# A language-model block on one core: FFN weights prepared in SBUF and turned by DMA in block 0, whose down products go by parts, with block 0's attention in slots of its own

## The reference

```python
h = rms_norm(rms_norm(emb_table[ids], norm_weight) @ proj_weight.T, None)
# attention, 16 heads of 32
z = layernorm(h)
q, k = feature_map(z @ Wq.T) * 32**-0.5, feature_map(z @ Wk.T)    # layernorm over 32, gamma, beta
v = z @ Wv.T
attn = where(causal, einsum(q, k) ** 2, 0)
h = h + (attn @ v / (attn.sum(-1) + eps)) @ Wo.T
# FFN, 2048 wide; fwht is the Walsh-Hadamard transform
x = fwht(layernorm(h) * SU_ug) / 64
x = silu(x @ W_gate.T * (Ws_gate * 64)) * (x @ W_up.T * (Ws_up * 64))
h = h + fwht(x * SU_dp) / 64 @ W_down.T * (Wscale_dp * 64)
```

## Time and profile before

| | |
|---|---|
| median of three executions | 1368.69 us |
| the profiled execution | 1369.22 us |
| its span, first to last instruction | 1367.4 us |
| mean granted TensorE clock | 0.970 |
| PE busy | 1258.8 us (92%) |
| DVE busy | 658.7 us (48%) |
| POOL busy | 565.2 us (41%) |
| ACT busy | 397.9 us (29%) |
| under 512 B, of 232708 DMA packets | 197893 |

### The profile page before, as it was taken

One profiled execution on the slowest core, in us unless ns is written; L12 is line 12 of the kernel. 1 busy time (PEld: TensorE's weight loads), 2 busy tenths in 40 slices (PEclk: granted clock), 3 DMA queues, 4 the chain that ended last, 5 costly groups with the idle time before them and its releaser, 6 DMA issues.

```text
span 1367.4 us, 18781 instructions
## 1 busy us (share of the span) xinstructions
PE 1258.8 (92%) x7257; PEld 620.6 (45%) x7257; DVE 658.7 (48%) x1154; ACT 397.9 (29%) x703; POOL 565.2 (41%) x483
## 2 busy tenths in 40 slices
PE   5565398999999999999999999999999999999999
PEld 3453054554444444444444444444444444444444
DVE  2654558782645363545455445534553644361110
ACT  5452354442133212330233113311331133211210
POOL 0443244342266424752375227632664266421210
PEclk9797699999999999999999999999999999999999
DMA  9912313311435234423444244333543445020000
GB/s 307 318 24 62 78 36 65 70 26 37 100 101 109 47 93 108 106 57 85 101 108 70 70 101 108 83 67 90 115 86 55 100 101 108 16 70 24 0 0 31
DMA packets 232708, 113.97 MB, mean 83 GB/s; under 512 B 197893, under 2 KB 215609, under 8 KB 232121
## 3 DMA queue, kind: packets, MB, share of 16 engines
q1 hardware_dynamic: 220160, 74.38, 25.7%
q0 software_dynamic: 11520, 37.76, 9.4%
q10 hardware_dynamic: 952, 0.75, 0.2%
HBM read 57.01 MB, written 9.70 MB: 49 GB/s over the span
## 4 chain that ended last, share of the span: by engine, by line
PE 77%; DVE 9%; DMA 4%; issue 4%; ACT 4%; POOL 1%; SPq 0%; DVEq 0%; POOLq 0%; ACTq 0%
PE bank L1178 23%; PE bank L1179 23%; PE bank L1180 23%; PE bank L1330 3%; DMA prod<-sg 2%; PE bank L1173 2%; DVE wd L568 1%; PE bank L1221 1%; DVE wd L567 1%; DVE wgu L553 1%; DVE prod L765 1%; PE bank L1171 1%; DMA hid<-in_L_tok_norm_weight 1%; PE bank L1339 1%; ACT wgu L951 1%
## 5 line engine op out<-in xcount | busy, mean ns | idle before, releaser
L1178 PE MATMUL bank<-xT,wgu 128*128 128x512 f16 x1024 | 389.8, 381 | 1.4 <-DVE xT L804 1.4
L1179 PE MATMUL bank<-xT,wgu 128*128 128x512 f16 x1024 | 389.8, 381 | 0.0
L1180 PE MATMUL bank<-xT,wgu 128*128 128x512 f16 x1024 | 389.8, 381 | 0.0
L470 POOL TENSOR_TENSOR hid<-a,hid 128x512 f16<-128x512 f32 x128 | 172.9, 1350 | 284.4 <-ACT hid L951 284.1
L839 DVE SCALAR_TENSOR_TENSOR a<-bank,kap,sg 128x512 f32<-128x512 f32 x128 | 96.1, 751 | 313.6 <-PE bank L1180 296.1
L1178 PE MATMUL bank<-wd,hid 128*128 128x512 f16 x512 | 194.1, 379 | 0.0
L1180 PE MATMUL bank<-wd,hid 128*128 128x512 f16 x512 | 194.0, 379 | 0.0
L1179 PE MATMUL bank<-wd,hid 128*128 128x512 f16 x512 | 194.0, 379 | 0.0
L951 ACT ACTIVATE hid<-a 128x512 f16<-128x512 f32 x128 | 80.9, 632 | 278.8 <-DVE a L839 278.8
L1180 PEld LDWEIGHTS bank<-xT,wgu 128*128 128x128 f16 x1024 | 100.5, 98 | 121.9 <-issue 2.0
L1178 PEld LDWEIGHTS bank<-xT,wgu 128*128 128x128 f16 x1024 | 100.8, 98 | 117.7 <-DVE xT L804 2.3
(11 more groups left out here) (192 smaller groups left out, 1371.1 us busy)
## 6 DMA issues: line engine op xcount, KB each, us to landing
out<-a SPq DMA_DIRECT2D x24, 256.0 KB, 2.2
wgu<-in_L_ffn_W_gate SPq DMA_DIRECT2D x16, 256.0 KB, 6.6
wgu<-in_L_ffn_W_up SPq DMA_DIRECT2D x16, 256.0 KB, 5.1
wd<-in_L_ffn_W_down SPq DMA_DIRECT2D x4, 1024.0 KB, 9.3
out<-h_row SPq DMA_DIRECT2D x8, 256.0 KB, 2.0
hid<-att_table,ids_p POOLq DMA_INDIRECT x84, 3.5
xT<-in_L_tok_proj_weight SPq DMA_DIRECT2D x1, 1024.0 KB, 7.3
p<-in_L_attn_Wq SPq DMA_DIRECT2D x1, 1024.0 KB, 11.9
```

Of the source, the lines that this page charges most:

```text
L470: nc.gpsimd.tensor_tensor(hid[:, 1, s, :], a32[:, :], hid[:, 0, s, :], ALU.subtract)\
L1178: mm(dst, w[0], v[0], start=first, stop=False)
L1179: mm(dst, w[0], v[1], start=False, stop=False)
L1180: return mm(dst, w[1], v[0], start=False, stop=final)
```

## The change

- **Loads.** One DMA per group of gate or up weights with 2 KB runs takes the place of four with 512 B runs. `norm_w` is asked for before the projection, and the down weights' first tile after all gate and up weights. The layout of `wgu` is new.
- **Start.** The squares and the sum for Wo and its turned units, and the values' product, move from before attention 0 into its slots. So do the first steps of `down_mix`, to behind its last slot. The first head's product waits for the first low table half alone (`att_low`), not for all four.
- **Attention 0** has SLOTS0 = 18 slots of its own. The four sums of heads are turned by eight PE transposes and one ACT copy (O_FLIP_AT0) and not by DMA. Behind slot 17, `tail` makes the Wo rows, the norms and the mixes of the four row tiles with nothing between them, and the rows too are turned on the PE (`x_flip`, `x_copied`).
- **Gate and up units.** 12 of 32 (TURNED) are still turned by PE, in slots 1 to 12 of attention 0, through three banks. The others are made in slots 0 to 9 of FFN 0, two per slot, with no PE work. ACT scales the f32 rows in place and copies the high half into one of three stage buffers (RING), POOL subtracts for the low half (`unit_low`), SP turns both halves by one DMA transpose straight into `wgu`. A unit waits until the DMA of three units before has landed. The PE waits for a slot's two units before it uses them.
- **Down units.** ACT makes the high half, DVE the low half, a DMA transpose on the same ring turns them, the PE makes the Hadamard product as two f16 matmuls (`down_hada`), and ACT and DVE split the result one slot later. They lie in slots 9 to 23.
- **Banks.** Gate has two banks in FFN 0 too, up has two up to slot 9 and one from slot 10 on.
- **FFN 0's down products** go part by part of the 2048 columns (outer) over the four row tiles (inner). The rows' last sums come in slots 29 to 31 and behind.
- **Attention 1** picks its heads by matmul as attention 0 does. Gathers begin with block 2.

```diff
-BEFORE = 16
-UNITS_IN_SLOT = (0, 0) + (1,) * BEFORE + (0,) * 14
-UNITS_BESIDE = 16
...
+RING = 3
+TURNED = 12
+UNIT_AT = tuple(range(1, 13))
...
+MIXED_BEFORE = 4
+MIX_BESIDE = (2, 3, 4, 5, 6, 7, 8, 8, 9, 10, 11, 12)
+SPLIT_BESIDE = (9, 10, 11, 13, 13, 13, 14, 14, 14, 15, 15, 15, 16, 16, 17, 18)
+HADA_BESIDE = (10, 11, 12, 14, 15, 16, 16, 17, 17, 18, 18, 19, 19, 20, 21, 22)
...
+HEADS_AT0 = (4, 8, 12, 16)
+O_AT0 = (5, 9, 13, 16)
+O_FLIP_AT0 = (6, 10, 14, 17)
+SLOTS0 = 18
...
+        def landed(x):
+
+            if x < TURNED:
+                return S["st_lo"], x + 1
+            return turning(x), 16 * ((x - TURNED) // RING + 1)
...
-                for i in range(4):
-                    rows_of_tile = w[512 * g + P * i:512 * g + P * i + P, :].rearrange("p (k d) -> p k d", k=DC)
-                    nc.sync.dma_start(raw[n][:, :, i, :], rows_of_tile).then_inc(S[f"gu_land{n}"], 16)
+                rows_of_tile = w[512 * g:512 * g + 512, :].rearrange("(i p) d -> p i d", p=P)
+                nc.sync.dma_start(raw[n], rows_of_tile).then_inc(S[f"gu_land{n}"], 16)
...
+            def unit_turn(x):
+                if x < UNITS:
+                    sp.wait_ge(S["st_low"], x - TURNED + 1)
+                else:
+                    sp.wait_ge(S["st_lo"], x - UNITS + TURNED + 1)
+                nc.sync.dma_start_transpose(unit_home(x), stage_of(x).rearrange("p l d -> p (l d)"))\
+                    .then_inc(turning(x), 16)
...
+            def unit_low(x):
+                pool.wait_ge(S["st_hi"], x + 1)
+                nc.gpsimd.tensor_tensor(stage_of(x)[:, 1, :], unit_raw(x), stage_of(x)[:, 0, :], ALU.subtract)\
+                    .then_inc(S["st_low"], 1)
...
                 feed(0, s)
+                for x in units_beside(s):
+                    unit_low(x)
                 product(1, s)
                 attend(1, s)
-                if s == NORM_BESIDE:
...
+            def unit_low(x):
+                dve.wait_ge(S["st_hi"], x + 1)
+                if x < TURNED:
+                    n, i = unit_place(x)
+                    nc.vector.tensor_tensor(wgu[:, n, i, 1, :, :].rearrange("p k f -> p (k f)"), TURN[x % 3][:, :],
+                                            wgu[:, n, i, 0, :, :].rearrange("p k f -> p (k f)"), ALU.subtract)\
+                        .then_inc(S["st_lo"], 1)
+                else:
+                    nc.vector.scalar_tensor_tensor(stage_of(x)[:, 1, :], unit_raw(x), unit_scale(x), stage_of(x)[:, 0, :],
+                                                   ALU.mult, ALU.subtract).then_inc(S["st_lo"], 1)
...
+            def tail():
+                for m in range(4):
+                    row_sum(0, m)
+                    if m:
+                        x_low(0, m - 1)
+                    if m > 1:
+                        xT_low(0, m - 2)
+                    row_norm(0, m)
+                    if m == 0:
+                        pair_norm(2)
+                        half_terms(0)
+                    if m == 1:
+                        pair_scale(2)
+                        bound_low(0)
+                    if m == 2:
+                        half_scale(0)
+                    if m == 3:
+                        pair_norm(3)
+                xT_low(0, 2)
+                x_low(0, 3)
+                down_mix(MIXED_BEFORE - 1)
+                xT_low(0, 3)
+                pair_scale(3)
...
+            for s in range(SLOTS0):
+                product(0, s)
+                if s < 2:
+                    att_low(2 + s)
+                if s == 2:
+                    val_low()
+                for x in units_before(s - 1):
+                    unit_low(x)
+                if s - 1 in WO_UNIT_AT:
+                    wo_low(WO_UNIT_AT.index(s - 1))
+                for x in units_before(s + 1):
+                    unit_diagonal(x)
+                attend_first(s)
+                if s == 5:
+                    pair_norm(1)
+                if s == 7:
+                    pair_scale(1)
+                if s == 8:
+                    wo_terms()
+                if s == 9:
+                    wo_total()
+                if s == 11:
+                    wo_fit()
+            for k in range(MIXED_BEFORE - 1):
                 down_mix(k)
...
+            def unit_high(x):
+                if x < TURNED:
+                    n, i = unit_place(x)
+                    act.wait_ge(S["turned"], x + 1)
+                    copy(wgu[:, n, i, 0, :, :].rearrange("p k f -> p (k f)"), TURN[x % 3][:, :]).then_inc(S["st_hi"], 1)
+                    return
+                if x >= TURNED + RING:
+                    act.wait_ge(*landed(x - RING))
+                else:
+                    act.wait_ge(S["wo_ready"], 1)
+                if x < UNITS:
+                    act.wait_ge(S["gu_scaled"], x // 8 + 1)
+                    copy(unit_raw(x), unit_raw(x), scale=unit_scale(x)).then_inc(S["st_scaled"], 1)
+                    act.wait_ge(S["st_scaled"], x - TURNED + 1)
+                    copy(stage_of(x)[:, 0, :], unit_raw(x)).then_inc(S["st_hi"], 1)
+                else:
+                    act.wait_ge(S["d_mix"], 4 * min(x - UNITS, 3) + 4)
+                    act.wait_ge(S["bound_done"], 1)
+                    copy(stage_of(x)[:, 0, :], unit_raw(x), scale=unit_scale(x)).then_inc(S["st_hi"], 1)
...
-                for v in down_evicts(2 * s):
+                feed(0, s, GATE[s % 2])
+                for x in units_beside(s):
+                    unit_high(x)
+                for v in down_hadas(s - 1):
                     down_unit(v)
-                for v in down_turns(2 * s):
-                    down_copy(v)
+                for v in down_splits(s):
+                    unit_high(UNITS + v)
                 feed_high(0, s)
-                for u in units_beside(2 * s + 1):
-                    unit(u, D_TURN)
-                for v in down_evicts(2 * s + 1):
-                    down_unit(v)
...
+            def down_hada(v):
+                if v and (HADA_BESIDE[v] < FT or v % 2 == 0 and HADA_BESIDE[v - 2] < FT):
+                    pe.wait_ge(S["d_lo"], v)
+                elif v > 1:
+                    pe.wait_ge(S["d_lo"], v - 1)
                 if v == 0:
...
+                pe.wait_ge(*landed(UNITS + v))
+                w = wd[:, DOWN_ORDER[v % 4], v // 4, :, :, :].rearrange("p l f d -> p l (f d)")
+                mm(D_HADA[v][:, :], hada16[:, :], w[:, 0, :], start=True, stop=False)
+                mm(D_HADA[v][:, :], hada16[:, :], w[:, 1, :], start=False, stop=True).then_inc(S["d_hada"], 1)
...
+                if first(n) and s in O_FLIP_AT0:
+                    q = O_FLIP_AT0.index(s)
+                    pe.wait_ge(S["ol_done"], QUADS * n + q + 1)
+                    bank = banks[6][:, :].bitcast(F16)
+                    for l in range(2):
+                        for m in range(4):
+                            c = (4 * l + m) * P
+                            last = nc.tensor.transpose(bank[:, c:c + P], o16[:, l, m * P:(m + 1) * P], ident16)
+                    last.then_inc(S["o_flipped"], 1)
...
+            def tail():
+                wo_rows(0, 0)
+                wo_rows(0, 1)
+                wo_rows(0, 2)
+                x_flip(0)
+                wo_rows(0, 3)
+                bound_sum(0)
+                for m in range(4):
+                    x_mix(0, m)
+                    if m < 3:
+                        x_flip(m + 1)
...
+            def feed_down_by_parts(s):
+                part, m = (s - FT) // 4, (s - FT) % 4
+                if m == 0:
+                    pe.wait_ge(S["al_done"], 4 * part + 4)
+                    pe.wait_ge(S["d_lo"], 4 * part + 4)
+                if part == 0:
+                    pe.wait_ge(*((S["silu_done"], FT - 1 + m) if m < 2 else (S["a_done"], FT) if m == 2 else (S["d_lo"], 5)))
+                down_rows(0, m, part)
...
+                    if s >= 2:
+                        pe.wait_ge(S["a_done"], s - 1)
+                    pe.wait_ge(*landed(2 * s))
+                    feed_half(s, 0, GATE[s % 2], S["gate_ready"])
...
+                    pe.wait_ge(*landed(2 * s + 1))
+                    if s > 10:
                         pe.wait_ge(S["a_done"], s)
-                    feed_half(s, 1, UP0, S["up_ready"])
...
+                    feed_down_by_parts(s)
+                for v in now:
+                    down_hada(v)
```

1035 lines of the change are left out of this document (538 added, 497 removed).

## The result

The changed kernel takes 1352.19 us (median of four executions, 1348.87 to 1354.19) and the kernel before, measured beside it, 1368.36. The ratio is 0.9881, with a 95% interval of 0.9860 to 0.9903: 1.2% faster, 16 us. The forecast was 1320 with a range of 1304 to 1347. The sign was right, the size was off by a factor of three, and the time lies outside the range.

The account below looks back on a forecast made before the run. PE-bound from 380.6 us on (986.8 us, unchanged); before that, chains of waits, then PE work in gate/up. 49.5 + 54.5 + 34.5 + 131.3 + 62 + 986.8 = 1318.6, with 1.8 outside the span 1320; range 1304 to 1347.

Parts of the forecast that it names:

- The ring: Gate/up of FFN 0: a unit waits for the DMA of three units before; this loop sets slots at 7.8 us.
- B: Rival, gate/up of FFN 0: the loop doesn't bind, ACT's 6.7 us sets the slots; 1311 us, chance 0.11.
- E: Rival, gate/up of FFN 0: DMA transposes are slow, trip 15.4 us, slower than before at 1381 us; chance 0.07.
- D: Rival, start and attention 0: the head start is lost, these stages take 56 and 60 us; 1332 us, chance 0.09.
- Rival C: Gate/up of FFN 0: POOL's two subtractions take about twice 1.16 us, trip 10.0; 1338 us, chance 0.17.
- The last of the forecast's signs: Middle of FFN 0: a clock of 0.50, where the PE now has gaps, would make all of stage 4 wrong.
- Stage 5: Down products of FFN 0: from 54.8 to 62 us, range 58 to 66.
- Stage 4: Gate/up of FFN 0: from 157.5 to 131.3 us, between 121 and 157.
- Stages 1 to 3: Start 64.5 to 49.5 us, attention 0 62.3 to 54.5, its tail 41.5 to 34.5.
- the values' f32 product, 3.7 us of PE: Start: this product moves behind the first heads, counted as 3.7 us off the path to the first head product.
- The 1 us for the loads: Start: `norm_w` in front of a 1 MB load and the new order of features, taken at 1 us more.
- 23 + 5 + 3.5: Tail of attention 0: 23 us for four row tiles, 5 for the first Wo product at half clock, 3.5 for the last turn.

Follow-up runs that it names:

- e2: Changed kernel with ACT's copy of the FFN product placed between the slot's two units, not behind both: 1343.37 us, ratio 0.9813 to the kernel before.
- e9: Changed kernel with the 12 later mixing steps working on 16 columns instead of 2048: 1347.24 us, ratio 0.9833 to the kernel before.
- e1: Changed kernel with the 12 later mixing steps placed two in each of slots 2 to 7 of FFN 0: 1355.73 us, ratio 0.9908 to the kernel before.
- e5: Changed kernel with POOL's gather of residual rows waiting for the turned heads' landing, not the first Wo product: 1348.96 us, ratio 0.9853 to the kernel before.
- e16: On the edits of e2, e4 and e5 joined (1339.30 us): slot 8's two mixes moved to slots 9 and 10, last four to 11, 11, 12, 12: 1337.37 us.
- e15: Changed kernel with 58 unused PE products ahead of the first Hadamard product in slot 10 of FFN 0: 1349.43 us, one profile.
- e3: Changed kernel with the norm weights loaded behind the projection again: 1359.66 us, one profile.
- e4: Changed kernel with DVE's step for the last weight norms moved behind the last row's low half in attention 0's tail: 1348.56 us, one profile.
- e13: Changed kernel with 40 unused PE products ahead of the first Hadamard product in slot 10 of FFN 0: 1357.29 us, one profile.

## Why the prediction was wrong

**The mechanism was right.** The ring binds the slots of FFN 0 (7.7 us measured, 7.8 forecast), through the chain that was named, and e2 shows it. That the two figures are so near is in part luck: without the mixes, which the forecast left out, a slot takes 7.5 (e9). The forecast also counts nine slots with units where the table has ten, and names 11 f16 pairs in this stage, where the table has five. All stages went the way that was said: three ahead of FFN 0 and gate/up shorter, the down products longer. The rest moved by 1.7 us in 985. Rivals B and E are out (slots of 7.7, landings of 3.2 us), and so is D, whose 56 and 60 for the first two stages were not reached. Rival C described a true effect, but too large for this order: without a mix beside them POOL's halves stay at 1.16, and even e1, with two mixes in a slot, took 8.9 us per slot and not C's 10.0. The last of the forecast's signs came in part: the clock of gate/up is 0.87, for 0.96 before, with half clock behind each long wait.

**Stage 5 failed as a term, 62 for 73.2.** The step was "the first part waits for the down units that came late, about 3; other waits 1". The PE idled 10.75 us (73.20 - 62.45). Each late unit's split stands in DVE's queue behind the row sums of attention 1, and these behind a gather. The forecast doesn't have that wait, which in the kernel before was harmless. The change put something behind it that the PE needs. e5 measures 4.8 us for it, 4.0 in the wait itself. The forecast also took every product at 0.2155 us: 58.1 us of work, for 62.45 busy. The 4.3 are half clock behind the waits; the stage's clock is 0.94.

**Stage 4 failed by 12.2.** The step was "In the new order the mix follows `product` and stands beside the second unit's or the head's subtraction, outside the loop, so I add nothing for it". e9 prices the mixes at 8.6, of which at most 3.0 are in the ring. The rule of the Trainium skill that I had beside it ("SBUF — State Buffer", SBUF: two separate sides) gave about 9. That its sum is so near is luck: it put 1.1 in each slot with a mix, and most of the cost lies behind the ring, in slots 8 to 12, where DVE's queue held the fit and two mixes ahead of the product. Silu 9 to 11 took 26.8 us, for two slots of 5.9 forecast. A second omission is the first down unit, for which I had no wait and which costs one of 12.5 us (8.9 with e2's edit, 4.4 with e16's, 6.6 without mixes). Behind it come 2 us of half clock (e15).

**Stages 1 to 3 failed by 9.7 together.** The start, 3.8: the failed step is the term "the values' f32 product, 3.7 us of PE", added to the 2.9 of ACT's squares. In the kernel before that product runs from 50.02 to 53.72, beside the squares (49.86 to 52.74) and the first score copy (52.75), so it was no link of its own. In the changed kernel that copy starts 2.6 us earlier, and from it to the first head product it takes 3.2 us instead of 11.8:

```profile
50.17 0.60 ACT L1185 ACTIVATE hid<-bank 128x512 f32<-128x512 f32 x1 [2.27 <-PE bank L1463]
...
53.34 0.69 DVE L863 TENSOR_TENSOR prod<-bank,cnt 128x512 f32<-128x512 f32 x1
```

That is 11.2 in all, for 15 forecast. Of the 8.6 behind the copy, 7.4 are the forecast's own terms for the mixing steps and the low halves, so at most 1.2 is left for the values' product. The 1 us for the loads is not seen (e3). Other profiles have the first head product at 51.0 to 52.8, so the size of this miss is not sharper than some 2 us.

Attention 0, 2.3: the last head's product came 42.9 us behind the first, 2.9 sooner than the 45.8 forecast. From it to the first Wo product it took 13.9 us for 8.7. The step that failed is the product's high half, taken as following at once. It stood 4.1 us in ACT's queue, behind a turned unit of Wo, for which ACT waited 2.09 us, and the copy of the turned heads before. Both came behind PE transposes that took 1.04 us, for 0.5 forecast:

```profile
96.22 0.68 DVE L863 TENSOR_TENSOR prod<-bank,cnt 128x512 f32<-128x512 f32 x1
...
97.00 1.04 PE L1525 MATMUL bank<-c,h_row 128*128 128x128 f16 x8 [3.23 <-POOL h_row L546]
...
99.51 1.01 ACT L1099 ACTIVATE oT<-bank 128x1024 f16<-128x1024 f16 x1
...
101.03 0.63 ACT L1099 ACTIVATE hid<-prod 128x512 f16<-128x512 f32 x1
```

The tail, 3.6: its terms as written, 23 + 5 + 3.5, add up to 31.5, and no row is named for the other 3.0 of the 34.5. Measured are 5.1 to the first row sum, 24.3 for the four row tiles (23 forecast), in which DVE waits 2.20 us for a bound that the PE sums behind the last Wo rows, and 8.7 from there to the first FFN product (6.5 with the unnamed 3.0). In the last stretch DVE's step for the last weight norms, taken as free, waits 2.63 us for ACT and costs 1.4 (e4):

```profile
142.14 0.17 DVE L636 TENSOR_SCALAR h<-h 128x8 f32<-128x8 f32 x1 [2.63 <-ACT hid L1096]
```

These readings of the three stages are of one trace, and only e4 tests one of them.

**The range** was made of single cases (a longer ring, a lost head start). Five stages that each miss by 2 to 12 us in the same direction were not one of them, and that is what came: a chain of waits was summed with each wait at its least.

## What to carry to other kernels

When a PE-bound stage is relieved of PE work, what is left is a train of small steps on four queues. Before costing it, write down for each queue what stands ahead of every step that the PE waits for; a wait that was harmless before (a gather ahead of a row sum) becomes the bound as soon as something the PE needs is put behind it. Count a PE wait like those of 4.2, 6.5 and 12.5 us here as itself plus some 2 us of half clock behind it. And look at the order inside a ring first: one copy moved by a place was worth half as much as the whole change.

## What was not expected of the hardware

- Steps of DVE on 128 x 1 to 128 x 4 values, 0.15 to 0.2 us by themselves, took 0.9 to 1.1 while POOL ran a subtraction:

```profile
221.66 1.12 DVE L719 TENSOR_TENSOR gl<-gl 128x1 f32<-128x1 f32 x1
222.82 0.17 DVE L720 RECIPROCAL gl<-gl 128x2 f32<-128x2 f32 x1
223.02 0.89 DVE L721 TENSOR_SCALAR gl<-gl 128x2 f32<-128x2 f32 x1
```

  Each of the long ones ends with POOL's operation, and the RECIPROCAL between them stayed at 0.17. The hold-up costs a tiny step about as much as a large one: 0.7 to 1.0 us here, 0.8 of a mixing step (1.22 to 2.06). By the Trainium skill ("SBUF — State Buffer", SBUF: two separate sides) it comes to operations with two inputs in SBUF and to those in a 2-port perf mode, for a whole instruction. The TENSOR_TENSOR agrees; which of the two holds for the TENSOR_SCALAR, with one tensor input, no run here shows.
- A transpose of eight 128 x 128 blocks by DMA landed in 3.2 us (median of 36). The estimate by the Trainium skill ("VectorE: DVE Perf Modes", The three transpose paths) had been 10.5.
- The PE ran at half clock behind a wait of 4.2 us that followed 8.8 us of unbroken work (e13).
- The same wait of 2.5 us in the down products was followed by full clock in 14 runs and by half clock in two (e3, e9), whose stage took 77.2 us. In e3 (0.58 for the first product behind it, where the changed kernel has 0.38):

```profile
344.51 0.58 PE L1552 MATMUL bank<-prod,hada 128*128 128x512 f16 x1 [2.54 <-DVE wd L680]
```
